# Splitting the query projection's operands into tiles that are loaded ahead and shared with the LoRA stage

## What is computed

```python
x = L0_attn_x                        # [2, 4096, 4096] float32
xn = _layernorm(x)
x = x + attn(xn, w_qkv, w_o) + ffn(xn, gate, kernel, bias, lora_A, lora_B, lora_A_shared, lora_B_shared)
# attn: 32 query heads, 8 key/value heads of 128, rotary embedding on q and k, causal softmax, output projection
# ffn:  xn @ kernel + bias + the LoRA terms: B_eff (A_eff xn) + B_shared (A_shared xn), A_eff and B_eff chosen by gate
```

## Time and profile before

| | us |
|---|---|
| median of the timed runs (2) | 4903.72 |
| lowest and highest of them | 4827.18, 4980.27 |
| the profiled execution | 4666.8 |
| its span, slowest core (core 5) | 4665.2 |
| spans of its other cores | 4594.1 to 4654.1 |

### The profile page before, as it was taken

The page is one execution under the profiler, slowest core; times in us unless marked ns, Lnnn a source line. Parts: engine busy times, 40 slices in busy tenths (PEclk is TensorE's granted clock), DMA queues, the critical chain, the costliest instruction groups (busy, mean ns, idle before and its releaser), DMA issues.

```text
span 4665.2 us, 46087 instructions; the slowest of 8 cores (4594.1 to 4665.2 us)
## 1 busy us (share of the span) xinstructions
PE 3759.7 (81%) x15376; PEld 1424.5 (31%) x15376; DVE 1428.3 (31%) x2642; ACT 982.9 (21%) x1041; POOL 537.3 (12%) x832
## 2 busy tenths in 40 slices
PE   4687787599984999378877878787788999299989
PEld 0233232244432444132222222222223444033334
DVE  0454434300101222114445454445442001022222
ACT  3111111000000000015655655565551000000000
POOL 1000000000000000012322222232320000000000
PEclk7888888799997999698888888888888999699999
DMA  9744441733327777601111111111116552856673
GB/s 142 124 105 102 88 84 52 150 93 95 103 60 116 91 97 99 125 25 37 46 37 41 41 43 41 37 42 40 43 37 104 101 102 57 175 112 132 138 134 93
DMA packets 398820, 394.71 MB, mean 85 GB/s; under 512 B 61952, under 2 KB 359168, under 8 KB 398464
## 3 DMA queue, kind: packets, MB, share of 16 engines
q0 software_dynamic: 214816, 223.94, 30.2%
q1 hardware_dynamic: 183776, 167.82, 12.3%
HBM read 470.30 MB, written 83.89 MB: 119 GB/s over the span
## 4 chain that ended last, share of the span: by engine, by line
PE 71%; DVE 10%; DMA 9%; another core or an unknown queue 5%; issue 3%; ACT 2%; SPq 0%; DVEq 0%; POOL 0%; ACTq 0%; POOLq 0%
PE kp L86 19%; PE w_p L86 9%; PE q_p L86 9%; PE a_av L86 8%; PE a_rw L81 7%; PE f_p L86 5%; DMA f_at<-sc_at 5%; PE a_s L86 5%; DVE a_rc L81 4%; PE a_s L81 4%; DVE kscr L81 2%; DMA lkv_x<-xTkv 2%; DVE f_s L81 1%; PE lp_pl L86 1%
## 5 line engine op out<-in xcount | busy, mean ns | idle before, releaser
L81 ACT ACTIVATE a_p<-a_s,p_btab 128x1024 bf16<-128x1024 f32 x768 | 815.1, 1113 | 1887.0 <-PE a_s L81 1887.0
L86 PE MATMUL f_p<-f_k,f_x 128*128 128x512 bf16 x2048 | 469.3, 389 | 131.5 <-DMA f_x<-sc_xkv 91.1
L86 PE MATMUL kp<-lkv_x,kv_w 128*128 128x512 bf16 x2025 | 461.8, 391 | 57.6 <-DVE lkv_x L81 35.7
L86 PE MATMUL q_p<-q_x,q_w 128*128 128x512 bf16 x1984 | 441.3, 381 | 79.5 <-DMA q_x<-sc_xkv 79.5
L81 DVE TENSOR_TENSOR a_w<-a_p 128x512 bf16<-128x512 bf16 x768 | 326.5, 425 | 584.0 <-ACT a_p L81 520.6
L86 PE MATMUL a_av<-a_p,a_v 128*128 128x512 bf16 x1536 | 482.1, 397 | 0.6 <-DVE a_p L81 0.5
L86 PE MATMUL kp<-kv_w,kv_x 128*128 128x512 bf16 x1984 | 440.0, 380 | 52.7 <-DMA kv_x<-sc_xkv 52.7
L86 PE MATMUL w_p<-w_w,p_attn 128*128 128x512 bf16 x1984 | 441.3, 381 | 8.3 <-DMA w_w<-woT 8.3
L81 PE MATMUL a_rw<-a_rc,p_onesf 1*128 1x512 f32 x128 | 122.0, 1051 | 292.8 <-DVE a_rc L81 292.8
L86 PE MATMUL a_s<-a_q,a_k 128*128 128x512 bf16 x768 | 314.5, 410 | 13.7 <-DMA a_k<-sc_k 10.1
L111 POOL DMA_DIRECT2D a_k<-sc_k x384 | 200.6, 525 | 1021.5 <-PE a_s L81 890.1
(11 more groups left out here) (91 smaller groups left out, 2173.6 us busy)
## 6 DMA issues: line engine op xcount, KB each, us to landing
lkv_x<-xTkv POOLq DMA_DIRECT2D x32, 1024.0 KB, 26.3
sc_xkv<-lkv_x SPq DMA_DIRECT2D x128, 256.0 KB, 2.6
kv_x<-sc_xkv SPq DMA_DIRECT2D x8, 4096.0 KB, 20.4
q_w<-wqT POOLq DMA_DIRECT2D x16, 2048.0 KB, 23.3
w_w<-woT POOLq DMA_DIRECT2D x8, 4096.0 KB, 28.6
f_k<-kern POOLq DMA_DIRECT2D x8, 4096.0 KB, 38.7
a_k<-sc_k POOLq DMA_DIRECT2D x384, 64.0 KB, 2.2
a_v<-sc_v POOLq DMA_DIRECT2D x192, 128.0 KB, 2.8
```

The costliest lines, as they stand in the source:

```text
L81: getattr(eng, m)(*aa, **kk).then_inc(s, st)
L86: getattr(eng, m)(*aa, **kk)
```

## The change

It does the following.

1. `q_x` (one tile of both chunks) becomes two tiles `q_x0` and `q_x1` of 512 tokens. `q_x0` is allocated before `kv_sweeps`, and its load is issued on SP by a hook in `kv_sweeps` at chunk 3. `q_x1` takes space that `kv_x` had, and is loaded on SP after the barrier that follows `kv_sweeps`.
2. `q_w` (two tiles of 256 columns) becomes `q_w0` and `q_w1` of 128 columns: one load per head (32 instead of 16), 4,096 rows of 512 bytes in HBM, 256 bytes in the tile. `q_w0`'s first load is issued on `gd` behind the 8 pieces of the value weights and ahead of the barrier before `kv_sweeps`; `gd` waits there for ScalarE, VectorE and all SP transfers so far. Inside `q_proj` the load for head h+1 is issued when PE is through with head h-1.
3. `q_proj`'s order: for each head of a pair both chunks are computed (before: for each chunk both heads). The PSUM tiles and the scratch tiles are those of the key stage (`kp`, `kscr` 0 to 5). There is now one set of scratch tiles, so the second `rope_block` of a pair waits for the stores of the first. cos and sin come into `kc` and `ks` in four loads.
4. `lp_aall` and `lp_as` are issued on `gd` at head 4 of `q_proj`, behind the load for head 5 and ahead of that for head 6.
5. `lora_pre` reads `q_x0` and `q_x1`: the second load of both chunks is gone.
6. `barrier` gets a parameter that no call uses, and `gd` waits once more for SP's transfers at the start of attention.

```diff
+    def q_proj(xqh0, xqh1, wq0, pk, kcs, ksn, kscr, vq0, gq0, aall, asb, lg):
...
+            xv1 = [sy.dma(out=xqh1[:].rearrange("p (a t) -> p a t", a=32),
+                          in_=fview(sc_xkv)[:, :, 7 * CH:8 * CH])]
...
+            pe.waitd(vq0)
+            pe.waitd(xv1)
...
+            for pr in range(NH // 2):
+                pvt = [0, 0]
+                for idx in range(2):
+                    hp = 2 * pr + idx
+                    wi = hp % 2
+                    if hp + 1 < NH:
+                        ni = (hp + 1) % 2
+                        gd.wait(s_pe, wdep[ni])
+                        gv[ni] = gd.dma(
+                            out=wq[ni][:].rearrange("p (a o) -> p a o", a=32),
+                            in_=fview(i_wqT)[:, :, (hp + 1) * 128:(hp + 2) * 128])
+                    if hp == 4:
+                        lg.append(gd.dma(out=aall[:].rearrange("p (a r) -> p a r", a=32),
+                                         in_=fview(i_aall)))
+                        lg.append(gd.dma(out=asb[:].rearrange("p (a r) -> p a r", a=32),
+                                         in_=fview(i_asT)))
+                    pe.waitd(gv[wi])
+                    for tc in range(2):
+                        pb = pk[2 * tc + idx]
+                        pe.wait(s_ve, pdep[2 * tc + idx])
...
+                for tc in range(2):
+                    b0, b1 = pk[2 * tc], pk[2 * tc + 1]
+                    ve.wait(s_pe, pvt[tc])
+                    ve.wait(s_ve, rdep)
+                    ve.waitd(sdep)
+                    c2, v6, s2 = rope_block(
+                        b0, b1, kcs[tc][:], ksn[tc][:], kscr[0:6],
...
     def kv_sweeps(wsb, kscr, pk, xp, wv_deps, xv0, hook=None):
...
+                if tc == 3 and hook is not None:
+                    hook()
...
+        def q_prefetch():
+            vq0.append(sy.dma(out=xqh0[:].rearrange("p (a t) -> p a t", a=32),
+                              in_=fview(sc_xkv)[:, :, 3 * CH:4 * CH]))
...
+            gd.wait(s_ac, ac.ctr.v)
+            gd.wait(s_ve, ve.ctr.v)
+            for d in sy.frontier():
+                gd.wait(*d)
+            gq0.append(gd.dma(out=wq0[:].rearrange("p (a o) -> p a o", a=32),
+                              in_=fview(i_wqT)[:, :, 0:128]))
+            xv0 = sy.dma(out=xp[0][:], in_=fview(sc_xkv)[:, :, 0:CH])
+            barrier(gd_front=gdf, sy_front=syf)
+            kv_sweeps(wsb, kscr, pk, xp, wv_deps, xv0, hook=q_prefetch)
...
+        barrier()
+        q_proj(xqh0, xqh1, wq0, pk, kcs, ksn, kscr, vq0, gq0[0], aall, asb, lg)
+        barrier()
+        lora_pre(xqh0, xqh1, aall, asb, lg)
...
-            xv = [sy.dma(out=xq[:].rearrange("p (a t) -> p a t", a=32)[:, :, 0:CH],
-                         in_=fview(sc_xkv)[:, :, 3 * CH:4 * CH]),
-                  sy.dma(out=xq[:].rearrange("p (a t) -> p a t", a=32)[:, :, CH:2 * CH],
-                         in_=fview(sc_xkv)[:, :, 7 * CH:8 * CH])]
...
-                    gv[ni] = gd.dma(out=wq[ni][:].rearrange("p (a o) -> p a o", a=32),
-                                    in_=fview(i_wqT)[:, :, (pr + 1) * 256:(pr + 2) * 256])
```

More of the change, by code:

```diff
@@ L169, in build_program, with barrier @@
     bar_n = [0]
-    def barrier(gd_front=None, sy_front=None):
+    def barrier(gd_front=None, sy_front=None, skip_gd=False):
         for r in (pe, ve, ac):
@@ L185, in barrier @@
         sy.marks[id(s_bar)] = bar_n[0]
-        for r in (pe, ve, ac, gd):
+        for r in ((pe, ve, ac) if skip_gd else (pe, ve, ac, gd)):
             r.wait(s_bar, bar_n[0])
@@ L372, in rope_block, with kv_sweeps @@
         return c2, v6, [s1, s2]
-    def kv_sweeps(wsb, kscr, pk, xp, wv_deps, xv0):
+    def kv_sweeps(wsb, kscr, pk, xp, wv_deps, xv0, hook=None):
         with ExitStack() as ps:
@@ new lines, in lora_pre @@
+    def lora_pre(xqh0, xqh1, aall, asb, lg):
+        with ExitStack() as ps:
+            pp = ps.enter_context
+            pl = pp(nc.psum_tensor("lp_pl", [128, CH], F32))
+            pls = pp(nc.psum_tensor("lp_pls", [RANK, CH], F32))
+            xqh = [xqh0, xqh1]
+            pe.waitd(lg)
+            for nt in range(4):
+                for tc in range(2):
+                    for dc in range(32):
+                        pe.call("matmul", pl[:],
+                                aall[:, dc * NRTOT + nt * 128:dc * NRTOT + (nt + 1) * 128],
+                                xqh[tc][:, dc * CH:(dc + 1) * CH],
+                                start=(dc == 0), stop=(dc == 31), inc=(dc == 31))
+                    pv = pe.ctr.v
+                    ve.wait(s_pe, pv)
+                    vv = ve.call("tensor_scalar",
+                                 sb_axg[:, nt * TOWN + tc * CH:nt * TOWN + (tc + 1) * CH],
+                                 pl[:], sb_gnr[:, tc * 4 + nt:tc * 4 + nt + 1], None,
+                                 ALU.mult)
+                    pe.wait(s_ve, vv)
+            for tc in range(2):
+                for dc in range(32):
+                    pe.call("matmul", pls[:],
+                            asb[:, dc * RANK:(dc + 1) * RANK],
+                            xqh[tc][:, dc * CH:(dc + 1) * CH],
+                            start=(dc == 0), stop=(dc == 31), inc=(dc == 31))
+                pv = pe.ctr.v
+                ve.wait(s_pe, pv)
+                vv = ve.call("tensor_copy", sb_axs[:, tc * CH:(tc + 1) * CH], pls[:])
+                pe.wait(s_ve, vv)
@@ L629, in build_program @@
-    lora_pre()
+        xqh0 = plk(nc.sbuf_tensor("q_x0", [128, 32 * CH], BF16))
+        wq0 = plk(nc.sbuf_tensor("q_w0", [128, 32 * 128], BF16))
+        vq0 = []
+        gq0 = []
+        def q_prefetch():
+            vq0.append(sy.dma(out=xqh0[:].rearrange("p (a t) -> p a t", a=32),
+                              in_=fview(sc_xkv)[:, :, 3 * CH:4 * CH]))
+        with ExitStack() as psv:
+            xp = [psv.enter_context(nc.sbuf_tensor(f"kv_x{i}", [128, 32 * CH], BF16))
+                  for i in range(2)]
+            gdf = gd.frontier()
+            syf = sy.frontier()
+            wv_deps = []
+            for piece in range(8):
+                gd.wait(s_pe, kstate["wkfree"][piece])
+                wv_deps.append(gd.dma(
+                    out=wsb[:].rearrange("p (a o) -> p a o", a=32)[
+                        :, piece * 4:(piece + 1) * 4, :],
+                    in_=fview(i_wvT)[:, piece * 4:(piece + 1) * 4, :]))
+            gd.wait(s_ac, ac.ctr.v)
[7 more added lines that the diff above has]
+            kv_sweeps(wsb, kscr, pk, xp, wv_deps, xv0, hook=q_prefetch)
@@ L630, in build_program @@
+        xqh1 = plk(nc.sbuf_tensor("q_x1", [128, 32 * CH], BF16))
+        aall = plk(nc.sbuf_tensor("lp_aall", [128, 32 * NRTOT], BF16))
+        asb = plk(nc.sbuf_tensor("lp_as", [128, 32 * RANK], BF16))
+        lg = []
+        barrier()
+        q_proj(xqh0, xqh1, wq0, pk, kcs, ksn, kscr, vq0, gq0[0], aall, asb, lg)
+        barrier()
+        lora_pre(xqh0, xqh1, aall, asb, lg)
+    syf_q = sy.frontier()
     barrier()
```

30 lines of the change are left out of this document (added).

## The result

The ratio of the changed kernel to the kernel before is 1.0041, with a 95% interval of 1.0024 to 1.0058: 0.4% slower, some 19 us. The medians of all timed runs, 4790.41 us for the changed kernel (43 runs) and 4821.16 us for the kernel before (42 runs), mix executions at two levels of the granted clock, so their difference says nothing; the ratio compares executions at the higher level (median of the changed kernel there: 4682 us), and so does all that follows. The profiled execution of the changed kernel spans 4681.6 us on core 7, its slowest.

The account below looks back on a forecast made before the run. TensorE held 71% of the chain, with gaps between stages from loads; on core 5 -64 - 45 + 6 + 3 + 67 + 33 = 0 us, so the median 4903.72 stays, about 4900 us, range 4790 to 5020.

Parts of the forecast that it names:

- the sum of 0: Whole kernel on core 5: savings of 64 and 45 us cancelled by losses of 6, 3, 67 and 33 us.
- the hook: Value sweep: a second 4,096 KB load on SP ahead of the stores delays a cast, +3 us once (0 to 8).
- the load before the value sweep: Gap before the value sweep: q_w0's first load shares full DMA engines with the awaited chunk, +6 us (0 to 14).
- the main term: Query projection: one-head loads land at 17.3 us against 13.8 us of PE on core 5, +67 us (0 to 160).
- I carry the sum over as it is and say 4900: Whole kernel: the profiled 4666.8 us stays, and the zero sum is applied to the timed median of 4903.72 us.
- The gaps: Before the LoRA stage 72 to 8 us, saving 64; before the query projection 79.3 to 35 us, saving 45.
- straight line through 16.9 and 26.7: Query weight loads on core 0: extrapolating to 1,024 KB gives 12.0 us, hidden behind 13.8 us of PE.
- the first rival: Query projection: weight loads are hidden on core 5 too, landing below 13.8 us; -72 us, 4832 us; chance 0.22.
- The LoRA matrices: Query projection, head 4: on q0 they stand ahead of head 6's load, PE stands 35 us; +33 us (0 to 45).
- The second rival: Query projection: LoRA matrices cost nothing either, sharing the engines with load 6; -100 us, 4804 us; chance 0.13.
- The third: Query projection: load time follows packets, each load keeps 18.2 us of engine time; +95 us, 4998 us; chance 0.18.
- The rule of 512 bytes: Query weight loads: with 256 B rows, half the bytes would make a load no cheaper, giving 4998 us; trace spoke against.

Follow-up runs that it names:

- first pair: First profiles of the changed kernel and the kernel before, unedited: mean stage sums 4649.2 against 4625.4 us, query projection 537.8 against 444.6 us.
- repeated pair: Changed kernel and kernel before profiled again, unedited, beside each other on one chip: mean span 4618.3 against 4620.7 us.
- the experiment: Changed kernel with q_w0's first load issued after the value sweep: gap before the sweep 48.9 us (63.7), before the query projection 34.2 us (30.6).
- the repeated run: Changed kernel profiled once more, unedited: query projection 520.9 us, mean span 4618.3 us; the kernel before was also repeated, 4620.7 us.
- fat-rows run: Changed kernel with each query weight load inside the projection as 1,024 rows of 512 columns, not 4,096 of 128: query projection 471.7 us.
- first execution: First profile of the changed kernel, unedited: query projection 537.8 us (mean of 8 cores), span 4681.6 us on core 7.

## Where the prediction was right and where it was wrong

**The time.** It forecast no change, 4900 us; measured is 0.4% more than before, and 4682 us lies below the stated range. Two steps failed. The first is the sum of 0: the two terms of loads added to a busy place were sized too small, the hook (+3, measured +12) and the load before the value sweep (+6, measured +12 to +15), each explained below. Against them stands an error the other way in the main term, the steady waits of the weight loads (+67, measured +37). In the first pair the sum of the stages before attention is +16, in the repeated pair 0. That the forecast sum comes near the second is luck: its mis-sized terms cancel. The second step is "I carry the sum over as it is and say 4900": it puts a sum made for the profiled execution of 4666.8 us onto the median of two runs, 4903.72, where the median of 42 is 4821.16. The profiled span would have been the better foot.

**The gaps.** Right: 7.7 us forecast before the LoRA stage, 6.9 measured; 35 forecast before the projection, 30.6 measured, 33.5 on core 7. That fits the fair sharing of the engines between chunk and weights, which no run tested by itself.

**The hook: a step that failed by its size.** The mechanism was right (SP held by two long issues, late stores, a cast, PE), forecast +3, measured +12. The failing step is "a store behind them waits for their drain, about 25 us", from which cast 3 of the chunk was to come at 30 us. The chunk began at 1117.6; SP issued the two loads from 1121.7 on, was free for the second store only at 1151.0, and the stores landed at 1157.7, so the drain took 36 us instead of 25. The cast came at 40 us, and since PE wanted its tile at 27.6, each of the 10 us more fell straight on PE. The clock after the stand, some 2 us, was left out of the forecast.

**The gap before the value sweep.** Forecast +6, the added load's engine time of 14 us shared; measured 12 to 15 by the experiment. The failing step is "its engine time, 14 us, is shared": with the engines full, PE lost about the whole of the load's engine time (11.8 us by the measure above), not half of it.

**The weight loads: the main term, mis-sized.** Right that they can't be hidden behind 13.8 us and that a pair's can behind 27.6. Wrong in whom it strikes. On core 5 a landing of 17.3 us was forecast, on core 0 12.0, hidden; it is 14.3 to 15.4 us on all cores in the repeated run, and all cores wait. Two steps failed. The landing for core 0 was drawn as a straight line through 16.9 and 26.7; measured, half the bytes in the same number of rows land only 2 us sooner, though the engine time falls by the 4 us that core 5's line gave (16.0 to 11.8, forecast 4.3), and the fat-rows run shows that three quarters of the rows are worth 5. And the slow loads of core 5, on which the sum was built, did not come again (16.2 us), as the first rival allowed. The two errors point in opposite ways, too little for core 0 and too much for core 5; for the slowest core, which counts, the steady term was +67 and is +37 on the mean with the matrices out of the way. The clock's part was 0.4 us a wait, not 1.3: most waits were of 1 to 3 us, and cost little after. The prediction called itself wrong altogether if core 5 was not the slow one in the timed runs, and it was not: of the 21 runs behind the 4682 us it was the slowest core in two, and each other core was the slowest in two to five.

**The LoRA matrices.** Forecast +33, measured +31 to +40, and +56 against the first execution. That they stand in the way of the weights was right, and so was the landing of load 6, forecast 67 us after the issue of load 5, measured 62 to 70 on the eight cores. But load 5, ahead of them, came late already (18 to 34 us instead of 17.3), GpSimd could not issue load 6 before that landing, and on most cores PE stood more than once. The second rival (they cost nothing) fell. The third (time follows the packets, 4998 us) was half right: at equal bytes, fewer and longer rows are much cheaper, but a load of half the bytes needs 11.8 us of the engines, not the 16.0 of the old one, so the stage did not turn into one of a load per 18 us.

**The rule of 512 bytes.** The Trainium skill, "DMA: Bandwidth & Descriptors", section Specifications, puts line rate at transfers from 512 B on. The runs agree in the direction: rows of 256 B reach 1,024 KB in 11.8 us of engine time, rows of 1,024 B in 7.2, with a quarter as many of them. A penalty that would make the load of short rows as dear as the old one, as the rival had it, did not show (11.8 us against the old load's 16.0 on core 0 of the repeated run and 18.2 on core 5 of the first).

## What to carry to other kernels

- Loads may be cut smaller only as far as the work that covers one still outlasts its landing; here half the columns halved the cover (27.6 to 13.8 us) and took 2 us off the landing. A cut by rows would fare better (1,024 rows landed after 9.3 us), but here it would need another order of the computation, which was not tried.
- A gap of loads before a stage is first to be asked whether the data are not on the chip already: keeping two chunks, with the weights fetched ahead by the pair, gave 64 and 61 us with nothing paid inside the stages, the changed kernel's prefetches 39 and 60 with 100 paid for them.
- A prefetch goes behind the queue's urgent work and in pieces that fit between it: 4,096 KB in one issue ahead of the stores cost 12 us, in eight issues behind them nothing.
- Before one core's landing time carries a forecast, it is to be seen in a second execution: 23.3 us became 16.2.

## What the runs showed that was not expected

GpSimd stood 29.1 us without a named releaser before it issued load 6, with load 5 and both LoRA matrices (3 x 4,096 rows) outstanding, and went on 0.3 us after the first of them had landed. With fat rows load 7 was issued while three loads were outstanding (both matrices and load 6, 2 x 4,096 + 1,024 rows), 13.8 us after load 6 on every core and so as soon as PE was through. It is not the number of loads alone, then, that makes GpSimd wait; where the bound in rows lies was not tried further.

The landing time of the same load differs between executions and cores: 23.3 and 16.2 us on core 5 of the kernel before, and a projection of 563 or 520 us on core 2 of the changed one. The slow cores were neighbours in both first profiles (4 and 5, then 2 and 3); why was not tried. The kernel before hides this scatter behind 27.6 us of PE; the changed one does not.
